# Where VectorE's round begins and ends: the loop boundary moved ahead of the first gated product

## What is computed

```
x = x + 0.5 * ffn(layernorm(x))       # "call 0" in the kernel
x = x + attn(layernorm(x)) @ weight   # 16 heads of 16 features, full 512 x 512 softmax
x = x + 0.5 * ffn(layernorm(x))       # "call 1", same weights as call 0
```

```
q, k, v = split(shift_token(x) @ wqkv)           # 256 -> 3 x 512, 8 heads of 64
q, k = rotary(l2norm(q) * qs), rotary(l2norm(k) * ks)
x = x + local_attention(q, k, v) @ wo            # windows of 128 tokens, one window back
h = layernorm(shift_token(x)) * lg + lb
a, g = split(h @ w1 + b1)                        # 2 x 682
x = x + (a * gelu(g)) @ w2 + b2                  # the gated product, then 682 -> 256
```

## Time and profile before

| | |
|---|---|
| median of 3 runs | 3990.23 us (3989.36 to 3994.13) |
| profiled execution | 3999.0 us |
| its span, first to last instruction | 3997.3 us |
| busy: PE / DVE / ACT / POOL | 3751.3 / 2573.6 / 2228.3 / 2184.3 us |
| granted TensorE clock, mean | 0.986 |
| first branch of the four loops on DVE | 323.3, 888.6, 2929.7, 3494.6 us |

### The profile page before, as it was taken

How to read it: one execution, slowest core, us unless ns; L and a number is a source line. 1 busy time by engine, 2 the same in 40 slices (tenths; PEclk the granted TensorE clock), 3 DMA queues, 4 the chain that set the end, 5 groups by cost and what they waited for, 6 DMA issues and landing times.

```text
span 3997.3 us, 75744 instructions
## 1 busy us (share of the span) xinstructions
PE 3751.3 (94%) x23552; PEld 3063.5 (77%) x23552; DVE 2573.6 (64%) x7286; ACT 2228.3 (56%) x5232; POOL 2184.3 (55%) x2179
## 2 busy tenths in 40 slices
PE   4999999999999799999999999998999999999997
PEld 3777777777777688888888888876777777777776
DVE  5677667766776465565555555656776677766774
ACT  2655665566656455444444444446656665566554
POOL 3555555555655355555555555655555555555653
PEclk8999999999999899999999999999999999999999
DMA  4000001110100100000000010001010011100110
GB/s 141 16 30 27 18 18 51 49 35 24 33 28 29 46 27 22 1 17 7 12 17 2 17 44 1 17 2 50 25 32 18 18 47 53 35 24 24 35 32 25
DMA packets 119072, 114.75 MB, mean 29 GB/s; under 512 B 13181, under 2 KB 116233, under 8 KB 118793
## 3 DMA queue, kind: packets, MB, share of 16 engines
q1 hardware_dynamic: 118792, 111.44, 8.8%
HBM read 73.69 MB, written 29.36 MB: 26 GB/s over the span
## 4 chain that ended last, share of the span: by engine, by line
PE 80%; DVE 10%; issue 4%; POOL 2%; DMA 1%; ACT 1%; SPq 1%; DVEq 0%; POOLq 0%; ACTq 0%
PE psum L1357 20%; PE psum L1358 18%; PE psum L1359 18%; PE psum L1469 6%; PE psum L1479 5%; PE psum L1499 5%; PE psum L1604 3%; PE psum L1458 2%; DVE nrm L1117 2%; DVE nrm L1115 1%; PE psum L1552 1%; DMA nrm<-xmid 1%; PE psum L1517 1%; PE psum L1437 1%; DVE turned_qk L1025 1%
## 5 line engine op out<-in xcount | busy, mean ns | idle before, releaser
L683 POOL TENSOR_TENSOR ge_lo<-ge,ge_hi 128x512 fp32r<-128x512 f32 x512 | 716.2, 1402 | 550.7 <-PE psum L1359 306.4
L643 POOL TENSOR_SCALAR probs<-probs,rz 128x256 f32<-128x256 f32 (+1 forms) x1024 | 444.6, 454 | 526.9 <-DVE rz L1077 526.9
L883 ACT ACTIVATE ge<-psum 128x512 f32<-128x512 f32 x512 | 306.4, 598 | 631.8 <-PE psum L1604 631.7
L789 ACT ACTIVATE probs<-probs,nb,rq 128x256 f32<-128x256 f32 (+1 forms) x1024 | 575.9, 566 | 40.7 <-DVE nb L1071 40.0
L1249 DVE CAST ge_hi<-ge 128x512 fp32r<-128x512 f32 x512 | 244.7, 479 | 546.6 <-ACT ge L883 546.3
L1063 DVE CUSTOM_DVE_ANT_0 probs<-psum,mask 128x256 f32<-128x256 f32 (+1 forms) x1024 | 339.4, 387 | 288.4 <-PE psum L1469 262.7
L625 POOL TENSOR_TENSOR rinv<-ssq,minus_half 128x16 f32<-128x16 f32 x124 | 365.5, 2947 | 162.7 <-DVE ssq L1040 159.2
L1357 PE MATMUL psum<-wqkv_hi,hT_hi 128*128 128x512 f32 x768 | 335.0, 436 | 53.8 <-DVE turned_sin L1029 52.1
L770 ACT ACTIVATE squares<-psum 128x512 f32<-128x512 f32 x256 | 150.2, 599 | 355.8 <-PE psum L1359 234.5
L653 POOL TENSOR_TENSOR hid_lo<-gate,hid_hi 128x512 fp32r<-128x512 f32 x160 | 207.5, 1297 | 254.2 <-ACT hid_hi L821 254.2
L1358 PE MATMUL psum<-wqkv_hi,hT_lo 128*128 128x512 f32 x768 | 308.6, 402 | 0.0
(11 more groups left out here) (163 smaller groups left out, 10579.1 us busy)
## 6 DMA issues: line engine op xcount, KB each, us to landing
xnext<-stream SPq DMA_DIRECT2D x32, 512.0 KB, 4.6
xmid<-stream SPq DMA_DIRECT2D x32, 512.0 KB, 3.8
stream<-xmid SPq DMA_DIRECT2D x16, 512.0 KB, 2.9
nrm<-xmid SPq DMA_DIRECT2D x32, 224.0 KB
wbuf<-L_ffn_wqkv SPq DMA_DIRECT2D x8, 768.0 KB, 8.2
wbuf<-L_ffn_w SPq DMA_DIRECT2D x8, 682.0 KB, 4.4
x_all<-L_attn_x SPq DMA_DIRECT2D x8, 512.0 KB, 7.7
stream<-x_all SPq DMA_DIRECT2D x8, 512.0 KB, 3.9
```

The lines of the kernel that those rows point to most:

```text
L643: last = nc.gpsimd.tensor_scalar(pu, pu, rz[:, h, t:t + 1], 1.0, ALU.mult, ALU.mult)
L683: nc.gpsimd.tensor_tensor(ges[1][:, k % 4, :], ge[:, k % 4, :], f32(ges[0][:, k % 4, :]), ALU.subtract).then_inc(S["g_lo"], 1)
L789: last = nc.scalar.activation(pu, pu, ACT.Exp, bias=nb[:, h, t:t + 1], scale=rq[:, 0, t, h:h + 1], accum_out=zs[:, h, t:t + 1])
L883: nc.scalar.activation(ge[:, k % 4, :], RB[k % 2], ACT.Exp, scale=GSCALE, accum_out=gz[:, h, t:t + 1]).then_inc(S["g_exp"], 1)
```

## The change

```diff
--- before.py
+++ after.py
@@ -50,9 +50,9 @@
 
 
 
-DVE_STEPS = ("X0 -y2 X1 R0 X2 i0 R1 L0 X3 i2 -y3 R2 L1 -y4 X4 i1 R3 L2 X5 R4 L3 X6 X7 P0 R5 L4 P1 R6 +zl0 +zl1 L5 "
+DVE_STEPS = ("-y0 Y c3 -y1 X0 -y2 X1 R0 X2 i0 R1 L0 X3 i2 -y3 R2 L1 -y4 X4 i1 R3 L2 X5 R4 L3 X6 X7 P0 R5 L4 P1 R6 +zl0 +zl1 L5 "
              "-y5 +rq0 R7 +rk0 L6 +ss0 -F -e +rk1 +ss1 +rq1 L7 +c0 P2 f0 P3 f1 +rq2 +c1 +rk2 x +ss2 l +rk3 r +rq3 "
-             "j +ss3 nl0 nl1 B +c2 y0 f2 +Y +c3 y1").split()
+             "j +ss3 nl0 nl1 B +c2 f2").split()
 
 
 POOL_STEPS = ("-ul1 N0 -ul2 N1 N2 N3 -ul3 N4 -ul4 N5 N6 -ul5 N7 +d0 +p0 +b0 +p1 +b1 +d1 +b2 +d2 +p2 s +b3 +d3 +p3 "
@@ -76,6 +76,7 @@
               40: "+d2", 41: "+pq2", 42: "+pk2", 46: "+b3", 48: "+d3", 49: "+pq3", 50: "+pk3"}
 BEGUN_PE, BEGUN_ACT = {64: "S0", 66: "S1"}, {66: "E0", 68: "E1"}
 BEGUN_DVE, BEGUN_POOL = {65: "X0", 67: "X1", 69: "R0", 71: "X2 R1"}, {69: "N0", 72: "N1"}
+HEAD_DVE = {0: "Y c3"}
 AHEAD_ORDER = " ".join(AHEAD_PE.values()).replace("+", "").split()
 
 
@@ -1209,9 +1210,11 @@
                 some_steps(n - 1, False, True, 1)
 
             def a_round(n, prev=True, nxt=True, load=None, switch=None, final=0, layer=0):
-                some_steps(n, prev, nxt, None, load, switch, final, layer, table=left(DVE_STEPS, BEGUN_DVE, load))
+                some_steps(n, prev, nxt, None, load, switch, final, layer, 
+                           table=left(DVE_STEPS, {**BEGUN_DVE, **HEAD_DVE}, load))
 
             def last(m, final, call=call):
+                some_steps(m + 1, True, False, -1, final=final, layer=1, part=slice(0, 2))
                 if call == 0:
                     for pair in gaz:
                         V.memset(f32(pair[0][half_rows[1], :]), 0.0)
@@ -1220,17 +1223,17 @@
                     dve.wait_ge(S["g_in"], 16 * 2)
                     statistics(0, gx[0], "g_st", "g_mv")
                     variance(0, "g_mv", "g_var")
-                some_steps(m + 1, True, False, -1, final=final, layer=1, part=slice(0, 1))
+                some_steps(m + 1, True, False, -1, final=final, layer=1, part=slice(2, 3))
                 if call == 0:
                     normalise(0, gn, gx[0], "g_rs", "g_y")
-                some_steps(m + 1, True, False, -1, final=final, layer=1, part=slice(1, 3))
+                some_steps(m + 1, True, False, -1, final=final, layer=1, part=slice(3, 5))
                 if call == 0:
                     y_lo(0, 0)
-                some_steps(m + 1, True, False, -1, final=final, layer=1, part=slice(3, 4))
+                some_steps(m + 1, True, False, -1, final=final, layer=1, part=slice(5, 6))
                 if call == 0:
                     dve.wait_ge(S["pe_p"], 2 * UNITS * ROUNDS)
                     pack(0, 0, 0)
-                some_steps(m + 1, True, False, -1, final=final, layer=1, part=slice(4, None))
+                some_steps(m + 1, True, False, -1, final=final, layer=1, part=slice(6, None))
                 stage_end(dve, 1 + call)
 
             rounds(dve, call, start, a_round, first, last)
```

## The result

The changed kernel takes 3996.07 us (median of 20 runs, 3992.89 to 4005.35), the kernel before 3990.53 us beside it (20 runs, 3986.80 to 3997.68). The ratio is 1.0015, with a 95% interval of 1.0008 to 1.0022: slower by 5.5 us or 0.15%, 3.2 to 8.8 us by the interval. The prediction was 3989.1 us, 1.1 us less than before. The profiled execution took 4003.7 us with a span of 4001.9 us, against 3997.3 us.

What follows compares the result with a forecast made beforehand. PE was taken as the bound. Terms: -7.8 (fourth loop's stall) + 1.5 (delayed code) + 5.2 (`f2`) = -1.1 us, carried over to the median of 3990.23: 3989.1 us, range 3984 to 4000.

Steps and rivals of the forecast that it cites:

- rival B: Fourth loop: the body fits in three blocks after all, no refetch; -2.6 us, 3987.6 us; chance 0.08.
- The step on `f2`: Four load rounds: `f2` ahead of `y0` delays `a1` and `K3`, net 1.30 us each; +5.2 us, bounds 3.6 to 7.2.
- what may thin the cover: Fourth loop's new branch: load burst and a fetch ahead may delay its code; +1.5 us, bounds 0 to 24.
- d: Extra delay of the code fetch behind the fourth loop's new branch; taken as 0.4 us, bounds 0 and 4.9.
- The cover of `y0`: Fourth loop: first record at 3490.5, `y0` waits for `a0` until 3491.24 anyway, so the first stall is hidden.
- the priced wait: Fourth loop: `K3` waits behind `c3`, whose code is in the second block; late by d - 0.1 us, five times.
- -7.8: Fourth loop: `X0` starts with `S0`'s end and 1.56 us a round go, 5 x 1.56 = 7.8 us.
- Rival A: Fetch behind the fourth loop's new branch: burst and fetch ahead delay the code, d = 2 us; +6.9 us, 3997.1; chance 0.30.
- the burst: Fourth loop: loads of `xnext` and `nrm` fill the DMA engines at the new branch; waiting it out costs 4.9 us.
- the fetch ahead: Fourth loop: the tail enters its fourth block six records before the branch, so another fetch is likely under way; no separate size.
- The count of the body: Fourth loop: 269 records starting at 121, ending past 384; four blocks by 6 records, fitting with six fewer.

Runs made afterwards that it cites:

- 119: Changed kernel with 20 satisfied waits once at the head of the second load round, moving the second loop's body; five rounds cost 15.3 us more than in three blocks.
- 120: Changed kernel with 21 satisfied waits once at the head of the second load round, moving the second loop's body; five rounds cost 7.3 us more than in three blocks.
- 127: Changed kernel with nine instructions of satisfied waits at the head of the last load round, putting the fourth loop's body back at its old place; 4004.19 us, ratio 1.0035.
- 117: Changed kernel with 18 satisfied waits once at the head of the second load round, moving the second loop's body; five rounds cost 12.4 us more than in three blocks.
- 17 instructions: Changed kernel with 17 satisfied waits once at the head of the second load round: second loop's body in three blocks; ran once, only its windows were compared.
- twelve in the fourth loop: Changed kernel with twelve instructions of satisfied waits at the head of the last load round: fourth loop's body in three blocks; 3990.72 us, ratio 0.9999.

## Why the prediction was wrong

The cause was read rightly: the fourth body touches four blocks, its code is fetched anew each round, and neither is true of the others. The fetches stayed in the fourth loop alone, rival B did not come, and the first three loops kept their rounds. The step on `f2` was right in mechanism and nearly in size: 4.8 us of waits net of those gone at `K3`, against 5.2, with 8 us (4.4 to 11.6) timed.

The step that failed is **what may thin the cover**, with its term d = 0.4 us and +1.5 us. The stall behind the branch is not 3.1 + 0.4 but 4.5 to 5.1 us, so d was 1.4 to 2.0. The loss did not stand where the prediction priced it either. It let `y0` pass and put the loss at `K3`, behind `c3`; in the trace `y0` itself is late, by 0.9 to 1.5 us, and TensorE waits at `a1`. The cover of `y0` was counted from the end of `c2`'s wait (3487.4 to 3491.24, 3.84 us, which is what loop 2 shows from branch to `y0`), and the first record needs another 0.2 us to become `y0`: 3.1 fits, 4.5 does not. At `K3` nothing is lost, because the body starts at 118 and not at 121: ten of its records lie in the first block, `c3` among them. At 119 and 120, where `c3` stands in the second block, the priced wait is there, 4.9 us in five rounds. The loop cost 5.5 us where the forecast had left 1.5. The edges inside the round, where VectorE falls 0.37 us behind in one step, had no term at all; they make 1.6 of the 5.5 us.

Sum with the measured terms: -7.8 + 5.5 + 4.8 = +2.5 us, where the interval begins at 3.2. The profiled spans differ by 4.6 us, but they also hold stretches that vary between profiles of the same code: the two middle rounds of the attention stage took 633.6 to 642.3 us over the profiles taken. So one to three microseconds stay unplaced; part of them may be the third load round. That the measured 3996.07 us lies within the range of 3984 to 4000 is not a success of the forecast, for the time moved the other way.

Rival A had nearly the right end (+6.9, 3997.1 us), but its mechanism is shown in small part only. Its first half, the burst, is a minor part: cutting the loads returned 1.7 us. Its second, the fetch ahead, makes 0.5 us of the stall at most: at 127 it is out of the way and the first record comes 0.5 us sooner, at 120 it is out of the way too (5.1 us ahead of the branch) and the record comes after 4.5 to 4.7 us all the same. What makes most of it goes with the new order: in the changed kernel the branch is issued while `c2` is still to run, and the packet that it needs starts 2.0 us or more behind it at every place tried, with the loads cut 2.0 to 2.7; in the kernel before the branch follows `y1`'s start, and the packet starts 1.0 to 1.3 us behind it at both places. Why, no run here shows. Also open is why the first record comes after 5.7 to 6.0 us at 117 and 119 and after 4.5 to 5.1 us at 118 and 120; the rest of the difference in their costs is `c3`.

The count of the body was one off (268, not 269) and the start 118, not 121, with the same four blocks. Two instructions fewer and it would have fitted, not six.

## What to carry to other kernels

A loop whose every round begins with an "issue" gap of some microseconds, beside a twin loop without one, was here a matter of where its code lies: count the records of its body, and move it by a few instructions ahead of the loop before touching the order of the work. Moving the boundary to hide such a stall exchanges one cover for another, and a stall measured at one place does not keep its size at the next: ask also which step stands behind the edge to the second block. A step that goes along with a move, as `f2` did, needs its own price, and its due time as well as its ready time.

## What the runs showed of the hardware

- VectorE's code is fetched in blocks of 128 instructions (8 KB); a loop over three blocks ran without a fetch, and one over four fetched five blocks a round. The step from one to the other is a single instruction, 12.3 us in five rounds.
- The same four-block loop cost 3.8 to 15.3 us for five rounds, depending on its place, on what stands around the branch and on the loads.
- Behind the first record, the second block came another 2.3 to 2.7 us later where the code reached it at once. At the edge to the third block VectorE fell behind by 0.37 us in one step. The step moves with the place (130th record of the body in the kernel before at 127, 139th at 118 in both orders, 140th at 117), and the bodies in three blocks that were compared (17 instructions; twelve in the fourth loop) have none.
- The attention stage's loop, 878 records long, is one more case in both kernels: its first record comes 2.8 to 3.1 us behind a taken branch.
- At the places tried, the code packet wanted by a branch started 1.0 to 1.3 us behind it in one order and 2.0 to 4.0 us in the other, and the first record came some 1.8 to 2.6 us behind the packet.
